# A quantised FFN on one NeuronCore: rounding offset carried through fp32 transposes, conversions off GpSimd, VectorE's order rewritten

## The chip, the cores and the metric

One Trainium2 chip, one of its cores. The metric is device time in microseconds of one execution of the whole program; lower is better.

## The reference, cut to what matters

Two batches of 512 tokens, width 128. Four residual steps follow each other: a cross attention to a context of 77 rows (16 heads of 64), a quantised gated FFN, a second transformer block (`a1`, causal self attention with 16 heads of 32, its own FFN, then `a2`, a second cross attention with its FFN) and a last FFN with a gate. The change is in the FFN of the first block and in what comes right behind it:

```python
def _act_quant(x):
    scale = 127.0 / jnp.clip(jnp.max(jnp.abs(x), axis=-1, keepdims=True), 1e-05)
    xq = jnp.clip(jnp.round(x * scale), -128.0, 127.0) / scale
def _bitlinear(x, w):            # weights are rounded to -1, 0, 1 times a mean
    return einsum('bsi,oi->bso', _act_quant(x), _weight_quant(w))
gate = silu(_bitlinear(x, w_gate)); up = _bitlinear(x, w_up)
out = _bitlinear(gate * up, w_down)
...
x = x + tanh(g_ffn[0]) * _L0_ffn_ref(_layernorm(x), w_gate, w_up, w_down)
x1 = _ln(_layernorm(x), ln1_g, ln1_b)      # then a1: xn = _ln(x1, lnx_g, lnx_b), yn = _ln(x1, lny_g, lny_b)
```

## The kernel before

Every engine has an instruction order written out by hand; semaphores join them. Tokens lie on the 128 partitions in four tiles (NT) per batch (NB = 2), so the quantised FFN has eight hidden tiles of 128 tokens by 512. PSUM has eight banks, S0 to S3, T0, T1, A and B. `claim` makes TensorE wait until the last reader of a bank is done, `await_bank` lets a reader wait for its filling, `release` marks it read.

Rounding is done by adding MAGIC = 1.5 * 2^23, which leaves an integer plus that offset in fp32.

**x of the FFN.** VectorE normalises (`ln_norm("f0", b)`) and takes the largest magnitude (`scale_x`, L1549). ScalarE multiplies by its inverse and adds MAGIC (`round_x`, L1115, four instructions of 128x128), then subtracts it into bf16 (`x_to_bf16`). TensorE transposes in bf16 (`xq_transposes`), ScalarE copies the result out (`xq_evac`). For batch 0 this happens at the end of the cross attention `cross("l0")`, whose 16 units run in a loop over i with the units' steps at i, i+1, i+2 and i+3; for batch 1 inside the FFN.

**Hidden tile n.** TensorE: `gate_up(n)`, two matmuls of 128x512 into the bank pair S0, S1 (n even) or S2, S3 (n odd). ScalarE: `silu(n)`. VectorE: the product with the up half into `h_in` (L1597), its largest magnitude (L1606), clip (L1602) and inverse (L1609); clip and inverse of tile n-1 stand in between those of tile n. ScalarE: scale and MAGIC (L1213). GpSimd: MAGIC off, to bf16 (L1021). TensorE: four bf16 transposes into T0 or T1 (L688). ScalarE: copy out (L1209). TensorE: four matmuls with `w_down` into A (batch 0) or B (batch 1) (L680). VectorE: `f0_out(b)`, scale and residual (L1566), for batch 0 before tile 7.

**Behind it, batch 0.** VectorE: statistics of ln1, affine norm in two passes of four instructions (L1357, L1361), statistics and norm of a1 (L1348). The variance's power is on GpSimd (`power`, L988). TensorE: `ln_transposes("a1", 0)` into A; ScalarE evacuates it twice, with the affine of x and of y (`a1_evac`); four projections of two matmuls (L711), whose high halves ScalarE takes (L1224) and low halves VectorE (L1628); the halves go through DMAs into `stack`, in the order in which the heads need them. Four value projections (L784) follow, then the attention loop over 32 heads: scores (L725), maximum (VectorE, L1691), exponential (ScalarE, L1265), mask of the diagonal block (GpSimd, L1032), transposes of the weights (L444), copies (L1250, L1655), values (L761). The second batch's `f0_out(1)` and ln1 statistics stand before the low halves, its affine norm (`ln1_gain`, `ln1_bias`, L1368 and L1375) before the loop, its a1 statistics and norm on VectorE inside it (n = 0 and n = 2).

`keep_busy(count, res)` (L460) issues matmuls of 128x512 that nobody reads, after waiting for the last reader of the bank `res`.

Of the kernel before, what the change touches and what calls it, by code (L numbers as in the profile page):

```python
# [33 lines left out]
BF16 = mybir.dt.bfloat16  # L34
# [48 lines left out]
def build(nc, x, ctx_in, w64, w128, wf0, wa1, wa2, wa2kv, wf1, rows, cols, out):  # L83
    with ExitStack() as st:
# [32 lines left out]
        def context_heads(start, n_tiles):  # L117
# [16 lines left out]
        xqb, xqT = (pring[:, s, k, :].bitcast(BF16).rearrange("p (b n) -> p b n", b=NB)  # L134
                    for s, k in ((0, 3), (1, 2)))
# [4 lines left out]
        hqb = hid[:, 1, 2:3, :].rearrange("p a n -> p (a n)").bitcast(BF16).rearrange("p (s n) -> p s n", s=2)  # L140
# [26 lines left out]
        rstd = sb("rstd", [P, NB, NT])  # L167
        cstats, cmv, cvar, crstd = (sb("cstats", [M, NB, 6]), sb("cmv", [M, NB, 2]),
# [55 lines left out]
        xq_ready, xqT_ready = sem("xq_ready"), sem("xqT_ready")  # L224
# [4 lines left out]
        hq_ready, hqT_ready = sem("hq_ready"), sem("hqT_ready")  # L229
# [210 lines left out]
        def _(pe):  # L440
# [6 lines left out]
            def ln_transposes(site, b):  # L447
                res = "AB"[b]
                claim(pe, res, ("ln", site, b), read_by=(ynT_ready, b + 1) if site == "a1" else
# [73 lines left out]
            def xq_transposes(b):  # L523
                pe.wait_ge(xq_ready, b + 1)
                res = ("A", "T0")[b]
                claim(pe, res, ("xq", b), read_by=(xqT_ready, b + 1))
                for t in range(NT):
                    m = pe.transpose(bank16(res)[:, t * P:(t + 1) * P], xqb[:, b, t * P:(t + 1) * P], identb[:, :])
                filled(m, ("xq", b))

            def cross(site):
# [5 lines left out]
                for i in range(NU + 3):  # L537
# [20 lines left out]
                    if site == "l0" and i == 2:  # L558
                        for n in range(len(VO_GROUPS)):
                            transpose_values("l0", 0, n, VO_BANKS["l0"][n])  # L560
                    if i >= 3:
# [33 lines left out]
                    if site == "l0" and i == NU + 1:  # L595
                        xq_transposes(0)
                        pe.wait_ge(wq_ready, 2)
                        gate_up(0)
# [68 lines left out]
            gate_up(1)  # L667
            for n in range(NB * NT + 4):
                if 1 <= n < NB * NT - 1:
                    gate_up(n + 1)  # L670
                if n >= 4:
                    j = n - 4
                    b, t = j // NT, j % NT
                    pe.wait_ge(hqT_ready, j + 1)
                    res = out_bank("f0", b)
                    if t == 0:
                        pe.wait_ge(wq_ready, 3)
# [1183 lines left out]
```

## Time and profile before

| | us |
|---|---|
| median of 3 runs | 370.52 |
| lowest and highest of them | 370.10, 373.45 |
| the profiled execution | 370.13 |
| its span, first to last instruction | 368.4 |

Busy over that span: TensorE 325.3, VectorE 287.4, ScalarE 271.0, GpSimd 122.7 us; mean granted TensorE clock 0.977. All durations below are from that one execution, and its time is 0.39 us below the median. PE is TensorE, PEld its weight loads, DVE VectorE, ACT ScalarE, POOL GpSimd, SP the queue that issues the DMAs; L1597 is line 1597 of the kernel. A bracket at a row's end is the engine's idle time before the row and what ended it.

### The profile page before, as it was taken

To read this page: it belongs to the slowest core of one execution; us is meant where nothing else is said; L and a number is where in the kernel's file an instruction comes from. 1 tells how busy PE (TensorE), PEld (TensorE's weight loads), DVE (VectorE), ACT (ScalarE), POOL (GpSimd) and SP (SyncE) were. 2 spreads that over 40 slices of the span, in tenths; PEclk is the share of its full clock that TensorE was granted. 3 is DMA by queue.
4 is the path that set the end of the run, shared out by engine and by line. 5 is a ranking of instruction groups with operands and counts; after the bars stand their busy time and mean duration, and the time that the engine had idled before them with its cause. 6 is when DMAs were issued, how large, how long until landed. Compare 5 with 4: busy or idle time off the path is not lost. (4 is left out here: it accounts for less than half of the span.)

```text
span 368.4 us, 6956 instructions
## 1 busy us (share of the span) xinstructions
PE 325.3 (88%) x2168; PEld 231.1 (63%) x2168; DVE 287.4 (78%) x738; ACT 271.0 (74%) x957; POOL 122.7 (33%) x227
## 2 busy tenths in 40 slices
PE   4989999636699788989989999989899899999997
PEld 4867988513344545655555566757566688877775
DVE  0768768787878998979898998985678887976545
ACT  2378899738445999999898999972545998892463
POOL 1316575324630332323232333331012454441110
PEclk9999999976799999999999999999999999999999
DMA  6900000000008969800992398400000000000001
GB/s 199 377 16 1 2 1 2 0 1 2 2 0 186 206 137 204 182 3 1 199 209 52 71 209 179 174 3 0 2 0 3 0 3 0 4 0 2 0 0 59
DMA packets 7052, 24.75 MB, mean 67 GB/s; under 512 B 1467, under 2 KB 1800, under 8 KB 6280
## 3 DMA queue, kind: packets, MB, share of 16 engines
q1 hardware_dynamic: 7016, 24.31, 27.4%
q8 instruction: 18, 0.29, 0.3%
q14 instruction: 18, 0.15, 0.1%
HBM read 7.00 MB, written 0.52 MB: 20 GB/s over the span
## 5 line engine op out<-in xcount | busy, mean ns | idle before, releaser
L1265 ACT ACTIVATE pring<-ps,nm 128x512 f32<-128x512 f32 x128 | 88.7, 721 | 6.7 <-DVE nm L1691 6.7
L1691 DVE TENSOR_REDUCE nm<-ps 128x1 f32<-128x512 f32 x128 | 80.9, 677 | 9.9 <-PE ps L725 9.7
L1144 ACT ACTIVATE arena<-ps,nmx 128x77 f32<-128x77 f32 x256 | 79.1, 346 | 11.4 <-DVE nmx L1443 11.1
L1032 POOL TENSOR_SCALAR_AFFINE_SELECT pring<-pring 128x128 f32<-128x128 f32 x128 | 37.2, 293 | 79.4 <-ACT pring L1265 79.4
L1144 ACT ACTIVATION_READ_ACCUMULATOR arena<-ps,nmx 128x1 f32 x256 | 58.2, 227 | 0.0
L725 PE MATMUL ps<-stack 128*128 128x512 f32 x128 | 53.4, 480 | 4.2 <-ACT pring L1265 3.6
L997 POOL TENSOR_TENSOR arena<-arena,rden 128x616 f32<-128x616 f32 x32 | 39.2, 1225 | 50.2 <-DVE rden L1452 50.2
L444 PE MATMUL ps<-ident,pring 128*128 128x128 f32 x320 | 47.6, 276 | 6.2 <-ACT early L1237 1.9
L444 PEld LDWEIGHTS ps<-ident,pring 128*128 128x128 f32 x320 | 36.2, 140 | 22.0 <-POOL pring L1032 11.7
L571 PEld LDWEIGHTS ps<-arena 128*128 128x128 f32 x320 | 38.9, 191 | 12.6 <-DVE arena L1459 11.2
L571 PE MATMUL ps<-arena 128*128 128x128 f32 x320 | 42.5, 280 | 3.3 <-DVE arena L1459 3.2
L988 POOL TENSOR_TENSOR rstd<-var,minus_half 128x4 f32<-128x4 f32 x18 | 19.1, 1062 | 76.9 <-DVE var L1341 76.8
L547 PE MATMUL ps<-arena,xnT 128*128 128x308 f32 x128 | 38.9, 427 | 1.7 <-ACT arena L1144 0.7
L725 PEld LDWEIGHTS ps<-stack 128*128 128x128 f32 x128 | 21.5, 189 | 25.5 <-ACT pring L1265 18.6
L1459 DVE COPY arena<-ps 128x384 f32<-128x384 f32 x64 | 28.2, 480 | 11.1 <-PE ps L444 11.1
L1250 ACT ACTIVATE arena<-ps 128x512 f32<-128x512 f32 (+1 forms) x48 | 28.4, 593 | 5.1 <-PE ps L444 5.1
L1443 DVE TENSOR_REDUCE nmx<-ps 128x8 f32<-128x616 f32 x32 | 25.5, 796 | 6.8 <-PE ps L547 6.4
L1265 ACT ACTIVATION_READ_ACCUMULATOR pring<-ps,nm 128x1 f32 x128 | 30.6, 239 | 0.0
L444 PE MATMUL ps<-ident,arena 128*128 128x128 f32 x200 | 27.5, 273 | 0.9 <-DVE arena L1419 0.5
L1168 ACT ACTIVATE hid<-ps,cols_sb 128x512 f32<-128x512 f32 x24 | 16.2, 685 | 15.6 <-PE ps L616 15.6
L1655 DVE COPY arena<-ps 128x384 f32<-128x384 f32 x48 | 26.2, 546 | 1.3 <-PE ps L444 1.2
L547 PEld LDWEIGHTS ps<-arena,xnT 128*128 128x128 f32 x128 | 21.7, 189 | 8.3 <-issue 1.9
(151 smaller groups left out, 527.3 us busy)
## 6 DMA issues: line engine op xcount, KB each, us to landing
stack<-sides SPq DMA_DIRECT2D x32, 256.0 KB, 5.2
stack<-arena SPq DMA_DIRECT2D x16, 256.0 KB, 5.0
stack<-hid SPq DMA_DIRECT2D x12, 256.0 KB, 5.3
wa_sb<-in_wa SPq DMA_DIRECT2D x1, 1536.0 KB, 13.5
early<-in_w SPq DMA_DIRECT2D x2, 512.0 KB, 7.7
stack<-hid SPq DMA_DIRECT2D x8, 128.0 KB, 2.5
arena<-in_wa SPq DMA_DIRECT2D x1, 1024.0 KB, 5.1
pring<-in_wf SPq DMA_DIRECT2D x1, 768.0 KB, 10.0
```

Of the source, the lines that this page charges most:

```text
L444: m = pe.transpose(bank(res)[0:width, t * parts:(t + 1) * parts], src(t), ident[0:parts, 0:parts])
L547: m = pe.matmul(bank(res)[:, 0:4 * HS].rearrange("p (h s) -> p h s", s=HS)[:, :, 0:M], xnT[:, b, t * P:(t + 1) * P], FK[:, b, c0:c0 + 4 * ...
L571: m = pe.matmul(bank(res)[:, t * P:(t + 1) * P], PTc[:, j % 4, k, :], VO[:, b, half * (NCH // 2) + k, :], start=(half == 0 and k == 0), st ...
L725: filled(pe.matmul(bank(f"S{i}"), stack[:, j, 0, e, i * P:(i + 1) * P], stack[:, j, 1, e, :], start=True, stop=True), ("s1", n, i))
L997: pool.tensor_tensor(pv, pv, rden[:, j % 4, :].unsqueeze(2).to_broadcast([P, 8, M]), ALU.mult).then_inc(pn_ready, 1)
L1032: pool.affine_select(out=blk, in_=blk, compare_op=ALU.is_gt, fill=0.0, base=0, pattern=[[1, P]], channel_multiplier=-1).then_inc(masked, 1)
L1144: ins = act.activation(Pc[:, i % PC_SLOTS, h * HS:h * HS + M], bank(where[key])[:, h % 4 * HS:h % 4 * HS + M], ACT.Exp, bias=nmx[:, i % 4, ...
L1250: release(act.activation(pt_piece(n, piece), src, ACT.Copy), key)
L1265: release(act.activation(pring[:, n % 2, i, :], bank(f"S{i}"), ACT.Exp, bias=nm1[:, n % 8, i:i + 1], accum_out=den1[:, n % 8, i:i + 1]), ( ...
L1459: release(dve.tensor_copy(PTc[:, j % 4, k0:k1, :].rearrange("p k n -> p (k n)"), bank(res)[:, 0:(k1 - k0) * P]), key)
L1655: release(dve.tensor_copy(pt_piece(n, piece), src), key)
L1691: dve.tensor_reduce(nm1[:, n % 8, i:i + 1], bank(f"S{i}"), AX.X, ALU.max, negate=True).then_inc(nm1_ready, 1)
```

## The change

- The offset stays: x and the hidden tiles keep MAGIC through transposes that are now fp32, from `xn` and `h_in`, and ScalarE takes it off in the copy out of PSUM, to bf16. `x_to_bf16` and GpSimd's L1021 go; the buffers `xqb` and `hqb` go.
- `round_x` moves from ScalarE to GpSimd: after j = 13 of `cross("l0")` for batch 0, after the power for batch 1.
- In `cross("l0")` VectorE does the second step of `l0_out(0)`, statistics, norm and scaling at i = 11, 12, 13, 14 instead of 12, 13 and 14, 15, 15; TensorE transposes x at the start of i = 16, and the first `gate_up` stands at the start of i = 17.
- The loop over hidden tiles is written out on each engine. VectorE: tile 6 behind ln1 and a1's statistics, tile 7 behind the a1 norm, `f0_out(1)` and its statistics behind the four low halves. TensorE: tiles 6 and 7 between the a1 transposes and the projections, `keep_busy` in other places.
- a1 norm of batch 0 is transposed twice, into A and S1; ScalarE evacuates x, VectorE y.
- GpSimd takes batch 1's ln1 norm with its affine (`ln1_affine`, six instructions and a negation of the mean) ahead of its first mask, and a1's norm of batch 1 behind head 2. VectorE's a1 statistics of batch 1 move from head 0 to head 1.

```diff
+            def hidden_transposes(n):
+                pe.wait_ge(hround_ready, n + 1)
+                res = f"T{n % 2}"
+                claim(pe, res, ("hq", n), read_by=(hqT_ready, n + 1))
+                transposes(("hq", n), res, lambda k: h_in[:, n % 4, k * P:(k + 1) * P], NF)
...
+            gate_up(2)
+            hidden_transposes(0)
+            keep_busy(3, "B")
+            gate_up(3)
+            f0_down(0)
+            hidden_transposes(1)
+            keep_busy(4, "B")
+            xq_transposes(1)
+            f0_down(1)
+            gate_up(4)
+            hidden_transposes(2)
+            gate_up(5)
+            hidden_transposes(3)
+            f0_down(2)
+            f0_down(3)
+            gate_up(6)
+            hidden_transposes(4)
+            f0_down(4)
+            gate_up(7)
+            hidden_transposes(5)
+            f0_down(5)
+            keep_busy(6, "S3")
...
+            hidden_transposes(6)
+            keep_busy(4, "A")
             ln_transposes("a1", 0)
-            keep_busy(4)
-            for m in range(4):
-                project(m, ("S0", "S2", "A", "B")[m])
-            for t, res in enumerate(("T0", "T1", "S1", "S3")):
+            claim(pe, "S1", "a1_context", read_by=(ynT_ready, 1))
+            transposes("a1_context", "S1", lambda t: xn[:, 0, t, :], NT)
+            f0_down(6)
+            project(0, "S0")
+            project(1, "S2")
+            hidden_transposes(7)
+            project(2, "S1")
+            f0_down(7)
+            project(3, "S3")
+            for t, res in enumerate(("T0", "T1", "A", "T0")):
                 project_values(t, res)
             keep_busy(6, "S0")
...
+            def round_x(b):
+                pool.wait_ge(xscale_ready, b + 1)
+                for t in range(NT):
+                    ins = pool.tensor_scalar(xn[:, b, t, :], xn[:, b, t, :], ainv[:, b, t:t + 1], MAGIC,
+                                             ALU.mult, ALU.add)
+                ins.then_inc(xround_ready, 1)
+            def negate_mean(site, b):
+                pool.wait_ge(var_ready, nth(site, b))
+                pool.tensor_scalar(nmean[:, b, :], mv[:, b, :, 0], -1.0, 0.0, ALU.mult, ALU.add)\
+                    .then_inc(nmean_ready, 1)
+            def ln_norm(site, b, src, dst):
+                pool.wait_ge(nmean_ready, negated[0])
+                pool.wait_ge(rstd_ready, nth(site, b))
+                for t in range(NT):
+                    ins = pool.tensor_scalar(dst[:, b, t, :], src[:, b, t, :], nmean[:, b, t:t + 1],
+                                             rstd[:, b, t:t + 1], ALU.add, ALU.mult)
+            def ln1_affine(b):
+                x1_b = x1[:, b, :, :]
+                ln_norm("ln1", b, r, x1).then_inc(ln1_step, 1)
+                pool.wait_ge(ln1_step, 1)
+                pool.tensor_tensor(x1_b, x1_b, row4("ln1_g"), ALU.mult).then_inc(ln1_step, 1)
+                pool.wait_ge(ln1_step, 2)
+                pool.tensor_tensor(x1_b, x1_b, row4("ln1_b"), ALU.add).then_inc(xn_ready, 1)
...
             power("f0", batches=[1])
-            for j in range(NB * NT):
-                pool.wait_ge(hround_ready, j + 1)
...
-                pool.tensor_scalar(hqb[:, j % 2, :], h_in[:, j % 4, :], MAGIC, None, ALU.subtract).then_inc(hq_ready, 1)
-                if j == 5:
-                    power("ln1", batches=[0])
+            round_x(1)
+            power("ln1", batches=[0])
             power("a1", batches=[0])
+            negate_mean("ln1", 1)
             power("ln1", batches=[1])
+            ln1_affine(1)
...
+            for n in range(7):
                 if n == 2:
                     xq_evac(1)
+                round_hidden(n)
+                if n + 2 < NB * NT:
+                    silu(n + 2)
+                if n < 6:
+                    hidden_evac(n)
...
+            ln_evac("a1", 0, ("a1_lnx_g", "a1_lnx_b"))
+            hidden_evac(6)
+            high_half(0)
+            high_half(1)
+            round_hidden(7)
+            high_half(2)
+            hidden_evac(7)
+            high_half(3)
+            copy_values(0)
             preload(ACT.Exp)
-            copy_values(0)
             copy_values(2)
...
+            hidden_behind(5)
+            hidden_scale_alone(5)
+            f0_out(0)
+            ln_stats("ln1", 0, r)
             ln_norm("ln1", 0, r, ("ln1_g", "ln1_b"), x1)
+            ln_stats("a1", 0, x1)
+            hidden(6)
+            hidden_max(6)
+            hidden_scale_alone(6)
+            ln_norm("a1", 0, x1)
+            hidden(7)
+            await_bank(dve, "a1_context")
+            release(dve.tensor_scalar(ynT[:, 0, :], bank("S1"), col("a1_lny_g"), col("a1_lny_b"), ALU.mult, ALU.add),
+                    "a1_context")
+            hidden_max(7)
+            hidden_scale_alone(7)
...
+            for m in range(4):
+                low_half(m)
             f0_out(1)
             ln_stats("ln1", 1, r)
-            for m in range(4):
-                low_half(m)
             copy_values(1)
             copy_values(3)
-            ln1_gain(1)
-            ln1_bias(1)
```

## Rows read from the trace of the kernel before

**Rows 1.** Windows: PE, PEld, DVE, ACT, POOL busy (instructions), clock, DMA share, GB/s.
```profile
...
80.00:90.00 10.00, 4.17 (x24) 2.09 (x23) 7.88 (x24) 7.43 (x15) 4.06 (x3) 0.55 0.00 0
90.00:100.00 10.00, 6.14 (x42) 2.94 (x43) 8.74 (x33) 6.30 (x11) 6.99 (x6) 0.79 0.01 3
...
120.00:130.00 10.00, 8.12 (x41) 5.04 (x39) 9.84 (x25) 8.80 (x25) 3.77 (x11) 1.00 1.00 211
...
```

**Rows 2.** Windows of 2 us, same columns.
```profile
...
78.00:80.00 2.00, 0.58 (x1) 0.10 (x1) 1.88 (x9) 0.00 (x0) 1.01 (x1) 0.69 0.01 4
...
96.00:98.00 2.00, 0.69 (x2) 0.28 (x3) 1.92 (x9) 0.00 (x0) 1.04 (x1) 0.50 0.00 0
...
102.00:104.00 2.00, 1.68 (x16) 1.17 (x16) 0.79 (x7) 0.60 (x1) 1.11 (x2) 0.83 0.00 0
...
```

**Rows 3.** Timeline of VectorE: start, busy time, line, operation, count, idle before.
```profile
...
76.36 0.75 DVE L1545 SCALAR_TENSOR_TENSOR r<-ps,tg,r 128x512 f32<-128x512 f32 x1
...
83.00 0.74 DVE L1597 SCALAR_TENSOR_TENSOR hid<-ps,du,hid 128x512 f32<-128x512 f32 x1
...
84.52 0.73 DVE L1597 SCALAR_TENSOR_TENSOR hid<-ps,du,hid 128x512 f32<-128x512 f32 x1
...
93.84 1.12 DVE L1566 SCALAR_TENSOR_TENSOR r<-ps,dout,r 128x128 f32<-128x128 f32 x4 [0.83 <-PE ps L680]
...
96.39 0.17 DVE L1341 TENSOR_SCALAR var<-mv 128x4 f32<-128x4 f32 x1
...
98.34 1.47 DVE L1357 SCALAR_TENSOR_TENSOR x<-r,mv,rows_sb 128x128 f32<-128x128 f32 x4
...
104.02 1.11 DVE L1348 TENSOR_SCALAR xn<-x,mv,rstd 128x128 f32<-128x128 f32 x4 [1.16 <-POOL rstd L988]
...
111.14 0.69 DVE L1628 SCALAR_TENSOR_TENSOR hid<-ps,hid 128x512 fp32r<-128x512 f32 x1 [0.17 <-ACT hid L1224]
...
114.55 1.13 DVE L1368 SCALAR_TENSOR_TENSOR x<-r,mv,rows_sb 128x128 f32<-128x128 f32 x4
...
116.89 2.48 DVE L1691 TENSOR_REDUCE nm<-ps 128x1 f32<-128x512 f32 x4
...
```

**Rows 4.** Timeline of TensorE, same columns.
```profile
...
95.27 0.40 PE L680 MATMUL ps<-wf0b,hid 128*128 128x128 bf16 x4 [1.03 <-ACT hid L1209]
95.52 0.40 PE L688 MATMUL ps<-identb,hid 128*128 128x128 bf16 x4
97.31 2.74 PE L464 MATMUL ps<-wf0b,identb 128*128 128x512 bf16 x6 [1.39 <-DVE hid L1597]
...
105.28 0.63 PE L444 MATMUL ps<-ident,xn 128*128 128x128 f32 x4 [0.37 <-DVE xn L1348]
...
106.77 1.12 PE L711 MATMUL ps<-xnT,wa_sb 128*128 128x512 f32 x2
...
109.45 1.02 PE L711 MATMUL ps<-ynT,wa_sb 128*128 128x512 f32 x2
...
114.85 1.27 PE L725 MATMUL ps<-stack 128*128 128x512 f32 x4
...
```

**Rows 5.** Timeline of GpSimd, same columns.
```profile
...
29.81 0.62 POOL L974 TENSOR_SCALAR bo_tg<-rows_sb,tg 128x128 f32<-128x128 f32 x1
...
36.05 1.27 POOL L979 TENSOR_TENSOR r<-r,bo_tg 128x512 f32<-128x512 f32 x1
...
41.31 0.69 POOL L963 TENSOR_SCALAR pring<-pring,winv 128x512 f32<-128x512 f32 x1
...
93.97 1.49 POOL L1021 TENSOR_SCALAR hid<-hid 128x512 bf16<-128x512 f32 x1 [0.18 <-ACT hid L1213]
...
102.95 1.04 POOL L988 TENSOR_TENSOR rstd<-var,minus_half 128x4 f32<-128x4 f32 x1 [0.88 <-DVE var L1341]
...
118.47 0.29 POOL L1032 TENSOR_SCALAR_AFFINE_SELECT pring<-pring 128x128 f32<-128x128 f32 x1 [9.10 <-ACT pring L1265]
...
```

**Rows 6.** Timeline of ScalarE, same columns.
```profile
...
105.94 0.78 ACT L1080 ACTIVATE xnT<-ps,cols_sb 128x512 f32<-128x512 f32 x1 [2.35 <-PE ps L444]
...
107.94 0.60 ACT L1224 ACTIVATE hid<-ps 128x512 fp32r<-128x512 f32 x1 [0.55 <-PE ps L711]
...
117.62 0.69 ACT L1265 ACTIVATE pring<-ps,nm 128x512 f32<-128x512 f32 x1 [3.93 <-DVE nm L1691]
...
121.41 0.69 ACT L1265 ACTIVATE pring<-ps,nm 128x512 f32<-128x512 f32 x1 [0.52 <-DVE nm L1691]
...
```

**Rows 7.** Waits in 66 to 120 us: total, times, longest.
```profile
...
PE ps L464 <- DVE hid L1597: 1.4, 1, 1.4
...
```

More of the change, by code:

```diff
@@ L523, in xq_transposes, with f0_down @@
             def xq_transposes(b):
[L524 to L529, printed above, removed]
+                pe.wait_ge(xround_ready, b + 1)
+                claim(pe, "AB"[b], ("xq", b), read_by=(xqT_ready, b + 1))
+                transposes(("xq", b), "AB"[b], lambda t: xn[:, b, t, :], NT)
+            def hidden_transposes(n):
[3 more added lines that the diff above has]
+                transposes(("hq", n), res, lambda k: h_in[:, n % 4, k * P:(k + 1) * P], NF)
+            def f0_down(n):
+                b, t = n // NT, n % NT
+                pe.wait_ge(hqT_ready, n + 1)
+                res = out_bank("f0", b)
+                if t == 0:
+                    pe.wait_ge(wq_ready, 3)
+                    claim(pe, res, ("out", "f0", b), filled_by=(f0_done, n + NT))
+                for k in range(NF):
+                    m = pe.matmul(bank(res)[:, t * P:(t + 1) * P], hqT[:, n % 2, k * P:(k + 1) * P],
+                                  wf0b[:, 2, k * P:(k + 1) * P], start=(k == 0), stop=(k == NF - 1))
+                filled(m, ("out", "f0", b))
             def cross(site):
@@ L560, in cross @@
                             transpose_values("l0", 0, n, VO_BANKS["l0"][n])
+                    if site == "l0" and i == NU:
+                        xq_transposes(0)
+                    if site == "l0" and i == NU + 1:
+                        pe.wait_ge(wq_ready, 2)
+                        gate_up(0)
                     if i >= 3:
@@ L1002, in cross @@
                         ternary((j - 5) // 2, (j - 5) % 2)
+                    if site == "l0" and j == 11:
+                        power("f0", batches=[0])
                     if site == "l0" and j == 13:
-                        power("f0", batches=[0])
+                        round_x(0)
                     if site == "a2" and j == 2:
@@ L1237, in copy_values @@
                 release(act.activation(V[:, t, :], bank(res), ACT.Copy), key)
-            def a1_evac(b):
-                ln_evac("a1", b, ("a1_lnx_g", "a1_lnx_b"), last=False)
-                ln_evac("a1", b, ("a1_lny_g", "a1_lny_b"), dst=ynT)
             def pt_copy(n, piece):
@@ new lines, in hidden_scale_alone, with hidden_behind @@
+            def hidden_scale_alone(n):
+                hidden_clip(n)
+                settle()
+                hidden_scale(n)
+            def hidden_behind(n):
+                hidden(n)
+                hidden_clip(n - 1)
+                hidden_max(n)
+                hidden_scale(n - 1)
+            hidden(0)
+            hidden_max(0)
+            hidden_scale_alone(0)
+            l0_out(1)
+            ln_stats("f0", 1, r)
+            hidden(1)
+            hidden_max(1)
+            hidden_scale_alone(1)
```

192 lines of the change are left out of this document (63 added, 129 removed).

## The prediction

> **What bounds the kernel now.** I read the windows first. From 120 us on, VectorE and ScalarE are 98% and 88% busy and TensorE 81% [rows 1]: the causal attention runs there, and its start is what everything behind it waits for. In the stretch that the change rewrites no engine is the bound: VectorE is 79% and 87% busy, ScalarE 74% and 63%, TensorE 42% and 61%, GpSimd 41% and 70% [rows 1]. There a chain from engine to engine decides, and TensorE's granted clock shows how idle it is: 0.69 in 78 to 80 us, 0.50 in 96 to 98, back to 0.83 in 102 to 104 [rows 2]. The profile's chain of what ended last only reaches back to 323 us, behind the change, so I followed the timelines, engine by engine, asking at each gap who was late.
>
> In them the middle reads so. VectorE adds cross attention's second batch into `r` at 76.36, paces tiles 2 and 3 of the hidden layer at 1.52 us each (83.00 to 84.52), starts `f0_out(0)` at 93.84, the affine norm of batch 0 at 98.34, the a1 norm at 104.02, the fourth low half at 111.14, batch 1's affine norm at 114.55, and only at 116.89 the first maximum of the attention [rows 3]. TensorE starts the a1 transposes at 105.28 and the fourth projection at 109.45, the first scores at 114.85 [rows 4]. GpSimd's conversion of a hidden tile takes 1.49 us [rows 5], nearly the 1.52 of VectorE, and sits between ScalarE and TensorE in every tile. The first exponential is at 117.62, the first of the second head at 121.41 [rows 6].
>
> I laid each engine's new order out with the durations of such rows, an instruction starting at the later of its engine being free and its last awaited result (0.06 us later). The old order laid out in the same way starts the a1 transposes at 105.26 (105.28 in the trace) and the second head's exponential at 121.39 (121.41), so the method is good to about 0.2 us. Times below are its results for the new order, on the clock of the profiled execution.
>
> **Cross attention's end.** VectorE does `l0_out(0)`, the statistics, the norm and the scaling each one turn earlier, in larger lumps, so the last maximum and the last exponentials are late by about 1 us; but `scale_x` no longer stands before the last reciprocal. The two nearly cancel. TensorE no longer waits there for the transposed x (ready at 69.8), so `hidden(0)` is at 73.4 and `l0_out(1)` at 75.2, 1.2 us earlier than the row at 76.36 [rows 3].
>
> **x of batch 1.** ScalarE's rounding and conversion become one rounding on GpSimd, 4 calls of 128x128. No row shows that call. The nearest by size is one multiplication of 128x128 at 0.62 us, the nearest by form (a scalar per partition and a constant, two operations, fp32) 128x512 at 0.69 [rows 5]. The mask, also 128x128, takes 0.29 [rows 5]. So 4 calls lie between 1.1 and 2.5 us; a second operation has not cost more in these rows, and I take 1.5, nearest to the form. It is on the path (the rounding starts at 81.7): `gate_up(4)` starts at 84.6, and 0.4 us earlier or 2.0 later by the ends for both batches.
>
> **Hidden tiles.** Without GpSimd's 1.49, tiles 4 and 5 follow ScalarE and TensorE; each fp32 quartet of transposes costs 0.6 us instead of 0.4 [rows 4] and is covered except in tiles 6 and 7. Tile 6 is moved behind the norm. `f0_out(0)` starts at 89.8, 4.0 us earlier. From there to the variance's end 2.72 us (93.84 to 96.56 in [rows 3]), to 92.6; the power on GpSimd 1.04 [rows 5], which is now bare, since VectorE's next instruction waits for it; the affine norm, two passes. Of such a pass the row at 98.34 shows 1.47 beside a busy GpSimd, the row at 114.55 1.13 beside an idle one [rows 3, 5]; it is now idle, so 2.3 instead of 3.0. Statistics 1.6 (2.72 less the 1.12 of `f0_out`), tile 6 alone 1.8 (the pace of 1.52 and the 0.3 that a following tile covered), so the a1 norm starts at 99.4: 4.6 us earlier than 104.02. Up to here the change gains.
>
> The Trainium skill (GPSIMD Engine Reference, section 8) says that GpSimd shares SBUF interfaces with VectorE and contends with VectorE instructions that have two SBUF inputs. The trace agrees, 1.47 against 1.13 for that pass; a reader without the page loses nothing of the sum.
>
> **TensorE ahead of the a1 transposes.** Here the gain is lost. `keep_busy(6, "S3")` waits for the last claim of S3, `gate_up(7)`, whose reader is `hidden(7)`; the trace shows that wait, 1.4 us, ended by VectorE's L1597 [rows 7]. The new order has `hidden(7)` behind the a1 norm: it ends at 101.2. TensorE has had nothing since about 94. A gap of that kind brought the clock to 0.50 [rows 2], and the six matmuls then took 2.74 us [rows 4]. So: 101.25 plus 2.6; the transposes of tile 6, queued behind, 0.9; `keep_busy(4, "A")`, 0.9 at the full clock and 1.7 at the low one. The clock came back about 5 us after the six began (97.31, and 0.83 in 102 to 104 [rows 2, 4]), so I take the middle, 1.3. The a1 transposes, ready at 100.5, start at 106.0, against 105.28: +0.7. The second set, into S1 for VectorE, costs 0.45 on TensorE and makes x and y land together.
>
> **From there to the first maximum.** Before: 105.28 to 106.77 to the first projection and to 109.45 to the fourth [rows 4], 1.5 and 2.7 us. After: `f0_down(6)` stands before the first projection and waits for `hidden_evac(6)`, itself behind `ln_evac`: 0.6 (the transposes) + 0.7 (`ln_evac`) + 0.6 (a copy out of a bank) + 0.2 (`f0_down`, whose end needn't be awaited), and the hand-overs, 2.3 us in all [rows 4, 6], to 108.3. Between projections 1 and 2 stand tile 7's transposes, which wait for two high halves and `round_hidden(7)`; between 2 and 3 stands `f0_down(7)`, which waits for `high_half(2)` and `hidden_evac(7)`. From the first projection to the fourth that is 6.1 us, to 114.4. The last low half starts at 116.1 (111.14 before). Then VectorE does what it did earlier before, `f0_out(1)` and statistics, 2.9 us, and two copies, 1.2; batch 1's affine norm (2.3) is gone from it. The first maximum is at 120.9, +4.0. The stack's DMAs start 5.4 us later with the halves that feed them; their slack to the third head (over 3 us) stays.
>
> **GpSimd's queue.** Behind `ln1_affine(1)` stand all masks, and TensorE's first transposes wait for a mask. The variance of batch 1 ends at 119.8; then the negation (128x4: between nothing visible and the power's 1.04, I take 0.35), the power 1.0, 4 calls at 1.5 (again 1.1 to 2.5), and two multiply-adds of 128x512 at 1.27 each [rows 5]. First mask 125.4, against 118.47. ScalarE's copy of the first transposes stands before its next exponential, so the second head starts at 126.9 instead of 121.41: +5.5. VectorE's statistics, moved into head 1, add 0.9 and the norm gone to GpSimd gives back 1.0 by head 4. From then on ScalarE is the bound, with the same work as before, so the shift stays for the rest: **+5.4 us**.
>
> **Sum.** 370.13 (the profiled execution, span 368.4) + 5.4 = 375.5. Its own time lies 0.4 below the median of 370.52, so the forecast is 375.9, 1.5% slower. About 1% is what a measurement of this kernel can tell from no change.
>
> **Rivals.**
> 1. *The keep-busy stretch is cheap.* If the clock is full at 101 us, both stretches and the transposes take 1.3 + 0.45 + 0.9: +3.2 in all, and with GpSimd's calls at 1.1 +2.3, so 372.8 to 373.7. Against it: more than 7 us without TensorE work. For it: little more than guesses on when the clock falls. Other sizes that I overrate by a third would land here as well. Chance 0.22.
> 2. *GpSimd's 128x128 calls cost as its 0.62 row.* +3.0 more (1.0 in each of the roundings and the norm): +8.4, so 378.9. For it: it is the only row of a 128x128 with a scalar per partition. Chance 0.10.
> 3. *The clock is already low from 80 us on.* TensorE now does the transposes in fp32 and two short keep-busy stretches between 76 and 84 us. If it falls as it did at 78 to 80, tiles 1 to 3 take 1.0 us longer: +6.4, so 376.9. The Trainium skill (TensorE: Matmul & The Clock Gate, Part 4) says that transposes do not count as busy in the way matmuls do, which would bring this case about; no row here separates the two. Chance 0.10.
> 4. *It is faster.* The 4.6 us won on VectorE reach the attention if TensorE's path from the norm to the first mask grows by less than that. Its terms are what stands between the norm and the transposes (5.5 us, with `keep_busy`), the hidden layer's steps between the projections (0.8 + 3.4 = 4.2) and GpSimd's lump. Without the first the forecast's +5.4 becomes about nothing, 370.4; with the second hidden as well it is 366.3. It decides at 4.3 us: below that sum of the two the kernel is faster, below 0.6 by over 1%. For it: TensorE, ScalarE and GpSimd have idle time in 90 to 100 us [rows 1]. Against it: each wait stands in a fixed order on its engine. Chance 0.06 for more than 1% faster, 0.05 for near no change.
> A conversion gone from GpSimd that buys nothing, as it is replaced by masks that wait, is part of my forecast and not a rival. My forecast as summed, +4.1 to +6.4: chance 0.47.
>
> **Chances and range.** Slower by over 1% (above 374.2): the forecast and rivals 2 and 3, 0.67. Within 1%: rival 1 and the rest, 0.27. Faster: 0.06. The range 371.2 to 380.0 leaves out the faster case and the worst joint price.
>
> **What would show it.** Right: `f0_out(0)` near 90, the a1 norm's end near 100.5, then the six keep-busy matmuls beginning at the end of `hidden(7)` near 101 at the low clock, the a1 transposes 5 us behind the norm, the fourth projection near 114, the first mask 6 us behind batch 1's variance, ScalarE waiting over 2 us between the first and second head's exponentials, and from the fifth head on the same pace as before. Wrong: a1 transposes within 1 us of the norm, projections 0.9 us apart, a first mask within 2 us of the first exponential, or 128x128 calls on GpSimd outside 0.28 to 0.62 us.

## The result, and the profile after

| | before | after |
|---|---|---|
| median, first measurement (4 runs each) | 371.68 us | 377.95 us |
| ratio, first measurement | | 1.017 (1.009 to 1.024) |
| median, measured again (17 and 4 runs) | 370.54 us | 377.54 us |
| ratio, measured again | | 1.019 (1.017 to 1.020) |
| profiled execution, span | 370.13, 368.4 us | 378.05, 376.3 us |
| busy TensorE, VectorE, ScalarE, GpSimd | 325.3, 287.4, 271.0, 122.7 | 330.3, 285.4, 267.0, 119.5 |

The kernel is 1.9% slower. The forecast was 375.9, 371.2 to 380.0. Four executions in a slower state (379.63 us in experiment 2, 372.95 in experiment 8, two of the kernel before) and three of 466, 789 and 1752 us are left out of the medians and ratios.

VectorE, ScalarE and GpSimd each have 2 to 4 us less work than before, and TensorE 5 us more, part of it at half the clock; the time grew by 6.3 to 7.0. The sum of an engine's work doesn't explain that; the timelines do.

The lines of after that answer to those of before follow, each engine's timeline with the same columns as before. VectorE, against [rows 3]:

```profile
...
74.87 0.75 DVE L1570 SCALAR_TENSOR_TENSOR r<-ps,tg,r 128x512 f32<-128x512 f32 x1
...
91.08 1.13 DVE L1592 SCALAR_TENSOR_TENSOR r<-ps,dout,r 128x128 f32<-128x128 f32 x4
...
94.92 1.14 DVE L1397 SCALAR_TENSOR_TENSOR x<-r,mv,rows_sb 128x128 f32<-128x128 f32 x4 [1.13 <-POOL rstd L1041]
...
100.55 1.10 DVE L1388 TENSOR_SCALAR xn<-x,mv,rstd 128x128 f32<-128x128 f32 x4
101.74 0.75 DVE L1623 SCALAR_TENSOR_TENSOR hid<-ps,du,hid 128x512 f32<-128x512 f32 x1
109.03 0.81 DVE L1683 TENSOR_SCALAR ynT<-ps,cols_sb 128x512 f32<-128x512 f32 x1 [6.54 <-PE ps L444]
...
118.05 0.69 DVE L1695 SCALAR_TENSOR_TENSOR hid<-ps,hid 128x512 fp32r<-128x512 f32 x1 [1.79 <-ACT hid L1263]
...
121.52 0.17 DVE L1381 TENSOR_SCALAR var<-mv 128x4 f32<-128x4 f32 x1
...
122.80 3.67 DVE L1754 TENSOR_REDUCE nm<-ps 128x1 f32<-128x512 f32 x6
...
```

Down to the a1 norm the change wins: `l0_out(1)` is 1.5 us earlier than in [rows 3], `f0_out(0)` 2.8, the a1 norm 3.5. Then comes the row of `ynT` at 109.03, with 6.54 us of idle time in front of it, ended by TensorE: VectorE waits for the a1 transposes. TensorE, against [rows 4]:

```profile
...
102.55 2.74 PE L464 MATMUL ps<-wf0b,identb 128*128 128x512 bf16 x6 [7.38 <-DVE hid L1623]
105.08 1.06 PE L444 MATMUL ps<-ident,hid 128*128 128x128 f32 x4
105.93 1.91 PE L464 MATMUL ps<-wf0b,identb 128*128 128x512 bf16 x4
107.64 1.35 PE L444 MATMUL ps<-ident,xn 128*128 128x128 f32 x8
109.91 0.40 PE L542 MATMUL ps<-wf0b,hid 128*128 128x128 bf16 x4 [0.92 <-ACT hid L1243]
110.15 1.08 PE L721 MATMUL ps<-xnT,wa_sb 128*128 128x512 f32 x2
...
113.38 0.66 PE L444 MATMUL ps<-ident,hid 128*128 128x128 f32 x4 [1.30 <-ACT hid L1235]
...
116.07 0.40 PE L542 MATMUL ps<-wf0b,hid 128*128 128x128 bf16 x4 [1.18 <-ACT hid L1243]
116.31 1.08 PE L721 MATMUL ps<-ynT,wa_sb 128*128 128x512 f32 x2
...
127.87 0.98 PE L444 MATMUL ps<-ident,pring 128*128 128x128 f32 x7 [2.35 <-POOL pring L1083]
...
```

The six matmuls that nobody reads (L464) start when VectorE's last hidden tile is done, after 7.38 us of idle time, at the low clock. Tile 6's transposes and four more unread matmuls follow, and only then the a1 transposes, at 107.64 (105.28 in [rows 4]). The projections, 2.7 us from first to last in [rows 4], take 6.2 here, with two waits for ScalarE between them (1.30 and 1.18) and one of 0.92 ahead of the first. Windows of 2 us over that place; the clock is the third number from the end:

```profile
...
102.00:104.00 2.00, 1.46 (x4) 0.58 (x5) 0.49 (x1) 0.00 (x0) 0.00 (x0) 0.50 0.00 0
104.00:106.00 2.00, 2.00 (x9) 1.24 (x7) 0.00 (x0) 0.00 (x0) 0.00 (x0) 0.50 0.00 0
106.00:108.00 2.00, 2.00 (x7) 0.98 (x6) 0.00 (x0) 0.00 (x0) 0.00 (x0) 0.50 0.00 0
...
```

In 104 to 108 us the other three engines do nothing at all, and TensorE works at half speed, for the most part on matmuls that nobody reads. GpSimd, against [rows 5]:

```profile
...
81.77 1.44 POOL L1005 TENSOR_SCALAR xn<-xn,ainv 128x128 f32<-128x128 f32 x4 [3.46 <-DVE ainv L1581]
...
121.79 0.20 POOL L1014 TENSOR_SCALAR nmean<-mv 128x4 f32<-128x4 f32 x1 [21.93 <-DVE var L1381]
121.94 1.01 POOL L1041 TENSOR_TENSOR rstd<-var,minus_half 128x4 f32<-128x4 f32 x1
123.13 1.74 POOL L1023 TENSOR_SCALAR x<-r,nmean,rstd 128x128 f32<-128x128 f32 x4 [0.18 <-POOL rstd L1041]
124.96 1.27 POOL L1032 TENSOR_TENSOR x<-x,rows_sb 128x512 f32<-128x512 f32 x1
126.30 1.26 POOL L1034 TENSOR_TENSOR x<-x,rows_sb 128x512 f32<-128x512 f32 x1
127.52 1.04 POOL L1083 TENSOR_SCALAR_AFFINE_SELECT pring<-pring 128x128 f32<-128x128 f32 x4
...
```

GpSimd waits 22 us for a variance, and then the whole of batch 1's affine norm stands ahead of the first mask, whose first exponential had come 4 us before. ScalarE, against [rows 6]:

```profile
...
123.52 0.69 ACT L1305 ACTIVATE pring<-ps,nm 128x512 f32<-128x512 f32 x1 [2.64 <-DVE nm L1754]
...
128.56 0.60 ACT L1285 ACTIVATE arena<-ps 128x512 f32<-128x512 f32 x1 [2.26 <-PE ps L444]
129.05 0.68 ACT L1305 ACTIVATE pring<-ps,nm 128x512 f32<-128x512 f32 x1
...
```

The second head's first exponential is at 129.05, 7.6 us later than in [rows 6]. The shift then stays: 7.43 us at the fifth head, 7.49 at the ninth, 7.56 at the 31st, and the span is 7.9 longer.

### The profile page after: what moved, and what is told of

The parts are those of the page before. It is cut to its first block and busy times, and to the rows that moved or that the text cites. A ratio compares the mean times of both kernels' runs of the same rounds, so it can differ in the third digit from the quotient of the medians.

```text
span 376.3 us, 6945 instructions
## 1 busy us (share of the span) xinstructions
PE 330.3 (88%) x2171; PEld 234.5 (62%) x2171; DVE 285.4 (76%) x727; ACT 267.0 (71%) x946; POOL 119.5 (32%) x239
## 5 line engine op out<-in xcount | busy, mean ns | idle before, releaser
L1305 ACT ACTIVATE pring<-ps,nm 128x512 f32<-128x512 f32 x128 | 89.7, 736 | 5.0 <-DVE nm L1754 5.0
L735 PE MATMUL ps<-stack 128*128 128x512 f32 x128 | 55.0, 491 | 1.8 <-ACT pring L1305 0.7
L1305 ACT ACTIVATION_READ_ACCUMULATOR pring<-ps,nm 128x1 f32 x128 | 32.6, 255 | 0.0
L1208 ACT ACTIVATE hid<-ps,cols_sb 128x512 f32<-128x512 f32 x24 | 16.2, 685 | 15.6 <-PE ps L634 15.6
```

The lines of the kernel that those rows point to most:

```text
L735: filled(pe.matmul(bank(f"S{i}"), stack[:, j, 0, e, i * P:(i + 1) * P], stack[:, j, 1, e, :], start=True, stop=True), ("s1", n, i))
L1305: release(act.activation(pring[:, n % 2, i, :], bank(f"S{i}"), ACT.Exp, bias=nm1[:, n % 8, i:i + 1], accum_out=den1[:, n % 8, i:i + 1]), ( ...
```

## The experiments

Each ratio is to the kernel before, run on the same chip, with its 95% interval. "Shift" is the start of the ninth head's first exponential in the profiled execution against before's 151.07. The times of several of these kernels spread over 4 to 5 us and the profile is of a single execution, so a shift says where in a trace the time went, and the median what the edit is worth.

**1. The six matmuls no longer wait for the last hidden tile.**

```diff
-            keep_busy(6, "S3")
+            keep_busy(6, "S2")
```

> The changed kernel with one edit: the six keep-busy matmuls behind tile 5 write bank S2 in place of S3, so they wait for silu(7) (about 94 us) and not for hidden(7) (102.5 us). Theory 1 (the fixed order on TensorE costs): tile 6's transposes start when round_hidden(6) ends, near 101.5 in place of 105.08, four keep-busy matmuls at the low clock follow, and the a1 transposes start near 104 in place of 107.64; the whole is 3.5 us shorter than the changed kernel, about 374.3. Rival (the low clock costs, not the order): without the six matmuls the array is cold for everything that follows, the projections take 1.72 us each in place of 0.86, and the gain is under 1.5 us.

Measured: 374.93 us, ratio 1.012 (1.007 to 1.017), shift +3.8. TensorE:

```profile
...
101.36 1.08 PE L444 MATMUL ps<-ident,hid 128*128 128x128 f32 x4 [5.02 <-issue]
102.24 1.91 PE L464 MATMUL ps<-wf0b,identb 128*128 128x512 bf16 x4
103.95 1.34 PE L444 MATMUL ps<-ident,xn 128*128 128x128 f32 x8
...
```

Nothing but the bank's letter is changed. The six now run in a gap at 95 us, and the a1 transposes come at 103.95 instead of 107.64. Of these 3.7 us about 1.1 are the wait itself (tile 6 was rounded at 101.4 in the first profile, and the six began at 102.55) and 2.5 the six matmuls at the low clock behind it. The theory had 3.5 us in all; the median is 2.6 to 3.0 below the changed kernel's, the shift 3.2 to 3.7.

**2. Neither the six nor the four.**

```diff
-            keep_busy(6, "S3")
...
-            keep_busy(4, "A")
```

> The changed kernel without the six keep-busy matmuls behind tile 5 and without the four behind tile 6. Theory 1: the a1 transposes start right behind tile 6's, near 102.4 in place of 107.64, 5.2 us earlier, and lose 1 to 2 us again because the first projections run at the low clock: 374 or 3 to 4 us less than the changed kernel, no better than with the six matmuls placed early. Rival (the clock decides): the low clock lasts into the value projections (3.6 us at the full clock), and less than 1.5 us is left.

Measured: 373.96 us, ratio 1.009 (1.006 to 1.012), shift +2.9, as the theory had it. TensorE:

```profile
...
101.92 1.09 PE L444 MATMUL ps<-ident,hid 128*128 128x128 f32 x4 [6.32 <-issue]
102.80 1.91 PE L444 MATMUL ps<-ident,xn 128*128 128x128 f32 x8
...
```

a1's transposes now run at the low clock, 1.91 us where experiment 1 had 1.34. That 0.6 us is less than the 1.91 of the four unread matmuls that should have raised the clock. 3 us of the loss are left without any of the ten.

**3. Batch 1's affine norm back on VectorE.**

```diff
-            negate_mean("ln1", 1)
             power("ln1", batches=[1])
-            ln1_affine(1)
...
             copy_values(3)
+            ln1_gain(1)
+            ln1_bias(1)
```

> The changed kernel with batch 1's ln1 norm and affine back on VectorE between the value copies and the attention loop, as before the change; GpSimd keeps batch 1's a1 norm. Theory 1 (lumps trade places): the first maximum is 2.3 us later (near 125.1 in place of 122.80), the first mask follows its exponential within 0.2 us, the second head's first exponential is near 128.4 in place of 129.05: 0.7 us gained, not to be told from nothing by the times. Rival (GpSimd's queue ahead of the masks is the main cause of the loss): 3 us or more gained.

Measured: 377.15 us, ratio 1.016 (1.013 to 1.020), shift +6.3, as the theory had it. GpSimd's lump is gone and the first mask (124.97) stands right behind the first exponential (124.11), but that exponential is late by VectorE's two passes. From the fourth projection to the second head's exponential it is 13.03 us, and 12.74 with the lump on GpSimd. Which engine does it is of no account; that it comes between the projections and the attention is.

**4. Tiles 6 and 7 ahead of everything of a1, on all engines.** TensorE's order; VectorE does `hidden(6)` and `hidden(7)` behind `f0_out(0)`, ScalarE its steps in the same order.

```diff
-            keep_busy(6, "S3")
+            keep_busy(2, "S2")
+            hidden_transposes(6)
+            keep_busy(2, "S2")
+            hidden_transposes(7)
+            f0_down(6)
+            f0_down(7)
+            keep_busy(4, "S3")
...
-            hidden_transposes(6)
-            keep_busy(4, "A")
             ln_transposes("a1", 0)
```

> The changed kernel with hidden tiles 6 and 7 on VectorE right behind ln1's statistics of batch 0 (ahead of its affine norm, where VectorE waited 1.13 us for the power), both tiles' TensorE steps ahead of the a1 transposes, and ScalarE in that order too; keep-busy matmuls split 2, 2 and 4. All else is the changed kernel's, the late f0_out(1) and GpSimd's affine with it. Theory 1: the a1 norm starts near 101.8 (1.2 us later than in the changed kernel, as tile 6 no longer covers the second power), but the a1 transposes start near 103 in place of 107.64 and the fourth projection 4.1 us behind them in place of 8.7; the first maximum is near 113.5 in place of 122.80, and the time is 9 us less: 369, 1 to 2 us under the kernel before. Rival (fp32 transposes or the low clock in 80 to 88 us are the cause): f0_out(0) and all behind it keep their lateness, under 3 us gained.

Measured: 370.35 us, ratio 0.999 (0.995 to 1.002), shift −1.0. The loss is undone, but the 1 to 2 us under the kernel before that were expected aren't there. TensorE:

```profile
...
103.00 1.07 PE L444 MATMUL ps<-ident,xn 128*128 128x128 f32 x8 [0.24 <-DVE xn L1383]
...
107.18 1.02 PE L727 MATMUL ps<-ynT,wa_sb 128*128 128x512 f32 x2
...
118.67 1.75 PE L444 MATMUL ps<-ident,pring 128*128 128x128 f32 x7 [2.33 <-POOL pring L1084]
...
```

The a1 transposes now start 0.24 us after VectorE's norm, and the fourth projection 4.2 us behind them instead of 8.7. The first exponential is at 114.33, 3.3 us earlier than in [rows 6], but the first mask (118.32) still stands behind GpSimd's affine norm, and most of the 3.3 is lost there: the second head's exponential is at 120.31, 1.1 ahead of before.

**5. The offset alone**, with every order as before: ScalarE still rounds x, VectorE does both affine norms.

```diff
-                pool.tensor_scalar(hqb[:, j % 2, :], h_in[:, j % 4, :], MAGIC, None, ALU.subtract)
...
-                        m = pe.transpose(bank16(f"T{j % 2}")..., hqb..., identb[:, :])
+                    transposes(("hq", j), f"T{j % 2}", lambda k: h_in[:, j % 4, k * P:(k + 1) * P], NF)
```

> The kernel before with one part of the change alone: x and the hidden tiles keep their offset through fp32 transposes, and GpSimd's conversion of the hidden tiles and ScalarE's of x are gone; every order is the old one, ScalarE rounds x, VectorE does both affine norms. My theory (the order and what stands between the engines decide, not the conversion): VectorE paces the hidden tiles at 1.5 us as before, f0_out(0) starts at 93.8 as before, the affine norm is no longer beside a busy GpSimd and gains 0.7, which TensorE's queue ahead of the a1 transposes swallows: a1 transposes at 105.3, second head's exponential at 121.4, time within 0.5 us of the kernel before (ratio 0.998 to 1.001). Rival (the conversion taken off GpSimd is itself worth something): a1 transposes 1 us or more earlier, time 1.0 to 1.5 us lower. Other rival (fp32 transposes are dear or let the clock fall): time 1 us or more higher, and the windows of 80 to 90 us at a lower clock than before.

Measured: 370.35 us, ratio 0.997 (0.994 to 1.000), shift +0.1; the second head's exponential at 121.49. VectorE's affine norm and a1 norm:

```profile
...
99.15 1.12 DVE L1335 SCALAR_TENSOR_TENSOR x<-r,mv,rows_sb 128x128 f32<-128x128 f32 x4
...
104.10 1.11 DVE L1326 TENSOR_SCALAR xn<-x,mv,rstd 128x128 f32<-128x128 f32 x4 [1.12 <-POOL rstd L981]
...
```

The pass is 1.12 us instead of 1.47 now that GpSimd is idle beside it, and from `f0_out(0)` to the a1 norm it is 9.45 us instead of 10.18. But `f0_out(0)` came 0.8 later than in [rows 3] and than expected (94.65), so the a1 norm is where it was. Tile 2 still started as before (83.05, 83.00 in [rows 3]); the 0.8 comes at tiles 4 to 6. VectorE can't write tile 4 before TensorE has transposed tile 0 out of the same buffer and waits 1.93 us there, where it waited 1.53 before, and the clock was at 0.50 up to 90 us, in the kernel before at 0.75 in 88 to 90. The two parts of this edit, the conversion taken off GpSimd and the transposes in fp32, are measured together only: as a pair, in the old order, they are worth nothing in time, so they don't make the changed kernel's loss by themselves. What each is worth alone isn't shown.

**6. `f0_out(1)` and its statistics ahead of y's copy**, on top of experiment 4.

```diff
             ln_norm("a1", 0, x1)
+            f0_out(1)
+            ln_stats("ln1", 1, r)
             await_bank(dve, "a1_context")
...
-            f0_out(1)
-            ln_stats("ln1", 1, r)
```

> The run with tiles 6 and 7 first on all engines (370.7), with f0_out(1) and its statistics also ahead of the evacuation of y on VectorE. In that run batch 1's variance ended at 112.3, GpSimd's affine norm followed, and the first mask at 118.3 stood 3.9 us behind the first exponential, TensorE idle 2.3. Theory (what still holds the attention back there is GpSimd's lump, which hangs on that variance): the variance ends near 107.5, the first mask comes down to 1 us behind the first exponential, y's copy is late by 2.9 us and moves the projections that need it and the first exponential by some 1 to 2 us, to 115.5 to 116.5; second head's exponential 117.5 to 119 (121.41 before), time 367.5 to 369. Rival (the projections' own chain is the bound, the lump hides): all of it comes later by what y's copy is late, second head at 121 or later, time 371 to 373.

Measured: 369.23 us, ratio 0.997 (0.995 to 0.999), shift −1.6. The variance ends at 105.6 and GpSimd's affine norm at 111.5, so the first mask (115.81) follows the first exponential (114.96) by 0.9 us, and the second head's exponential is at 118.11, 3.3 us ahead of before. Then a new wait takes half of it. TensorE, and windows of 2 us:

```profile
...
121.72 0.70 PE L741 MATMUL ps<-stack 128*128 128x512 f32 x2 [2.82 <-DMA stack<-hid]
...
```

```profile
...
120.00:122.00 2.00, 0.28 (x1) 0.30 (x2) 2.00 (x7) 1.89 (x6) 0.34 (x2) 1.00 0.97 234
122.00:124.00 2.00, 2.00 (x11) 1.78 (x10) 1.93 (x10) 0.85 (x2) 1.28 (x3) 0.61 1.09 223
124.00:126.00 2.00, 2.00 (x7) 1.28 (x6) 1.72 (x4) 1.80 (x6) 0.73 (x3) 0.53 0.92 188
...
```

The third head's scores need the stack's DMAs, which run at 0.97 of the 16 engines and can't start before the projections' halves. They are the bound of that head now, and behind the wait the clock was at 0.61 and 0.53. The lump's part of the theory holds; the time is a little above its 367.5 to 369, as this wait wasn't in it.

**7. `f0_out(1)` into the wait for a1's power, and batch 1's a1 statistics ahead of the attention**, on top of experiment 4; GpSimd's negation and power for them stand ahead of its masks too.

```diff
             ln_stats("a1", 0, x1)
+            f0_out(1)
             ln_norm("a1", 0, x1)
+            ln_stats("ln1", 1, r)
...
             copy_values(1)
+            dve.wait_ge(xn_ready, nth("ln1", 1))
+            ln_stats("a1", 1, x1)
             copy_values(3)
```

> The run with tiles 6 and 7 first, and besides: f0_out(1) between the statistics and the norm of a1 (it fills the wait for the power), the ln1 statistics of batch 1 right behind that norm, the a1 statistics of batch 1 ahead of the attention loop, and GpSimd's negation and power for them ahead of the masks. Theory: a1 transposes near 103.4, fourth projection near 107.8, batch 1's variance ends near 104.8, GpSimd's affine norm near 111, so the first mask stands right behind the first exponential (114.3) and the second head's exponential is at 117.4 (121.41 before). The third and later heads are limited by the DMAs of the stack and gain 3.9 us. Time 366.2 to 366.8, ratio 0.988 to 0.990. Rival (the DMAs of the stack or VectorE in the first heads eat it): second head near 117.4, but the ninth within 2 us of before, time 368.5 to 370.5.

Measured: 372.06 us (367.90 to 373.31), ratio 1.001 (0.997 to 1.004), shift +2.3. A miss: neither the theory's 366.2 to 366.8 nor the rival's second head near 117.4 (119.95) came. The profiled execution took 372.80 us, near the upper end of the twelve. `f0_out(1)` had to wait 1.15 us for `f0_down(7)`, and the a1 norm behind it left TensorE idle for 1.3 us (transposes at 104.20). The clock was 0.50 in 106 to 108 us, and the first two projections took 1.99 and 1.89 us, 1.12 and 1.02 in experiment 8. Behind that the wait for the stack was 4.2 us.

**8. The same with 5 and 6 unread matmuls instead of 3 and 4 behind tiles 0 and 1.**

```diff
-            keep_busy(3, "B")
+            keep_busy(5, "B")
...
-            keep_busy(4, "B")
+            keep_busy(6, "B")
```

> The kernel with f0_out(1) and the affine norm early, with 5 and 6 matmuls instead of 3 and 4 that nobody reads, behind the transposes of hidden tiles 0 and 1. Theory (in the changed kernel the granted clock fell to 0.50 in 82 to 86 us because TensorE idled there between short transposes, and that cost 1.3 us): the clock stays above 0.8 in 80 to 88, f0_out(0) comes 0.7 to 1.3 us earlier and all behind it with it, time 0.5 to 1.3 us below the kernel it is made from. Rival (the added matmuls stand in the way, or the clock falls for the gaps before 80 us): f0_out(0) at the same time or later, time the same or up to 0.6 us higher.

Measured: 369.64 us, ratio 0.997 (0.995 to 1.000), 2.4 below experiment 7 (the intervals of the two overlap), shift −2.6. The clock was 1.00 from 76 to 96 us, and `f0_out(0)` stood 15.1 us behind `l0_out(1)`, 15.6 in experiment 7: 0.5 us, where 0.7 to 1.3 were expected, and experiment 9 has the same 15.1 without the edit. The rest of the difference lies in the two profiled executions: in this one the clock was at 1.00 from 104 us on, ahead of the projections (1.12 and 1.02), and in experiment 7's it fell once more. That the edit does this isn't shown.

**9. The changed kernel again.**

> The changed kernel itself once more, beside five rounds of the kernel before, as its own four executions gave only 1.009 to 1.024. Expected 377.4 (376.0 to 378.5), a ratio of 1.014 to 1.022. In its trace the stretch from l0_out(1) to f0_out(0), whose text is the same in six kernels measured, took 15.1 to 16.2 us, by when the clock was low in it; here it falls in the same range, and the a1 transposes stand 7 us behind the start of the a1 norm in any case.

Measured: 377.54 us (377.05 to 377.59), ratio 1.019 (1.017 to 1.020), shift +7.0. Windows of 2 us, both of which were at 0.50 in the first profile of the same kernel:

```profile
...
82.00:84.00 2.00, 0.49 (x2) 0.12 (x2) 1.83 (x6) 0.13 (x1) 1.44 (x4) 1.00 0.00 0
84.00:86.00 2.00, 1.53 (x12) 0.86 (x13) 1.82 (x5) 1.43 (x3) 0.00 (x0) 1.00 0.00 0
...
```

**10. The changed kernel with the edit of experiment 8.**

> The changed kernel with 5 and 6 matmuls that nobody reads instead of 3 and 4 behind hidden tiles 0 and 1. Theory (the low clock in 80 to 88 us is one part of the error of the forecast, at most 1.1 us of its 2.1): from l0_out(1) to f0_out(0) 15.1 us instead of 16.2, the clock above 0.9 there, the stretch behind it unchanged (the six matmuls still wait for the last hidden tile, at the low clock), ninth head at +6.4 instead of +7.5 against before, time 0.5 to 1.1 us below the changed kernel's. Rival (the clock falls for something that these matmuls don't touch): 15.6 us or more, time the same.

Measured: 377.88 us (377.27 to 378.08), ratio 1.020 (1.018 to 1.021), shift +7.0. The stretch took 15.1 us, as it did in experiment 9 without the edit. So the clock there was no lasting cause, and the theory's gain of 0.5 to 1.1 us didn't come.

**11. Experiment 6 with the edit of experiment 8, and 8 unread matmuls ahead of the third head's scores.**

```diff
+                if n == 2:
+                    keep_busy(8, "S0")
                 if n < NHB:
                     scores(n, 0)
```

> The kernel with tiles 6 and 7 first and f0_out(1) ahead of y's copy (369.2), with 5 and 6 instead of 3 and 4 unread matmuls behind tiles 0 and 1, and 8 of them ahead of the third head's scores, where TensorE waited 2.8 us for a DMA of the stack. Theory (that wait let the clock fall to 0.53 in 122 to 126 us, and with it the gain of the ninth head over before shrank from 2.3 to 1.6 us): the clock stays above 0.9 in 120 to 128, second head near 118.5 (121.41 before), third near 123.6, ninth 2.4 to 2.8 us ahead of before, time 368.0 to 368.7, ratio 0.993 to 0.996. Rival (the DMAs of the stack hold the third head and the added matmuls only stand in their way): ninth head 1.6 us ahead or less, time 369 or more.

Measured: 368.83 us (367.63 to 371.80), ratio 0.996 (0.993 to 0.998), the lowest median of all, though its interval overlaps those of experiments 6 and 8; against the changed kernel's 377.54 it is 8.7 us less. Its mechanism isn't shown, though. The profiled execution, 370.22 us, lies in the upper part of the twelve, shift −0.4 where the theory had −2.4 to −2.8 and the rival −1.6 or less. TensorE in it:

```profile
...
118.84 1.90 PE L464 MATMUL ps<-wf0b,identb 128*128 128x512 bf16 x8
123.00 1.09 PE L741 MATMUL ps<-stack 128*128 128x512 f32 x2 [2.26 <-DMA stack<-hid]
...
```

The stack's data came at 123.00, 14.9 us behind the start of the fourth projection; in experiments 6, 7 and 8 that distance was 13.5, 14.9 and 13.5. The clock fell to 0.50 in 124 to 126 us in spite of the eight matmuls. Whether they or the two edits at tiles 0 and 1 make the 0.4 us between this median and experiment 6's can't be told.

## Why the prediction was right

The direction, the mechanism and the place of each loss are as predicted; the size was 1.4 to 2.2 us short by the two profiles, 1.6 to 2.1 by the medians. The band of the forecast as summed, +4.1 to +6.4, holds the first measurement (+6.3 against the kernel before measured beside it) and not the second (+7.0); the range held by its width on this side. Both profiles of the changed kernel against the chain of the prediction:

| start of | predicted | first profile | experiment 9 |
|---|---|---|---|
| `l0_out(1)` | 75.2 | 74.87 | 75.47 |
| `f0_out(0)` | 89.8 | 91.08 | 90.61 |
| a1 norm | 99.4 | 100.55 | 100.08 |
| a1 transposes | 106.0 | 107.64 | 107.01 |
| first projection | 108.3 | 110.15 | 109.20 |
| fourth projection | 114.4 | 116.31 | 115.36 |
| first maximum | 120.9 | 122.80 | 121.86 |
| first mask | 125.4 | 127.52 | 126.58 |
| second head's exponential | 126.9 | 129.05 | 128.25 |

- **The hidden tiles: the step that was too small.** From `l0_out(1)` to `f0_out(0)` I had 14.6 us; it took 16.2 with a low clock in 82 to 88 us and 15.1 at the full clock. So about half of the error was there before the a1 norm began. Part of it is the clock: rival 3 did occur in the first profile, for 1.1 us, and not in the second. The other 0.5 us is in both, and 0.4 of it comes ahead of batch 1's x: from `l0_out(1)` to GpSimd's rounding VectorE took 6.9 us, and the prediction had 6.5. Behind that VectorE waits for ScalarE's `silu` ahead of tiles 4 and 5, 0.95 and 0.85 us in the first profile and 0.27 and 0.44 in the second; the prediction had these two tiles follow ScalarE and TensorE, and at the full clock it is only 0.2 us off from the start of `gate_up(4)` to `f0_out(0)`. The Trainium skill (TensorE: Matmul & The Clock Gate, Part 4) would lay rival 3 to the transposes, which it says don't count as busy as matmuls do. The traces don't bear that out as the cause here: experiment 9 has the same fp32 transposes with the clock at 1.00 from 76 to 96 us. Whether transposes count less than matmuls no run here can show, as matmuls run between them in all these kernels.
- **The bare power and the affine norm.** Predicted 1.04 and 1.15 per pass, measured 1.13 of idle time and 1.14. The a1 norm begins 9.47 us behind `f0_out(0)` in both profiles; predicted 9.6. Experiment 5 shows the contention on VectorE gone with GpSimd's conversion (1.12 against 1.47).
- **TensorE ahead of the a1 transposes.** Six matmuls, tile 6 and four matmuls: predicted 4.8 us, of which the four were a middle between two clocks. Measured from the first start to the a1 transposes 5.1 in the first profile (clock 0.50 to the end) and 4.5 in experiment 9 (0.79 in the last window). The middle was fair, and rival 1, a full clock, is out. Experiment 1 takes the wait and the six matmuls out of this place and gives 2.6 to 3.0 us of time, experiment 2 takes the four out as well and gives 3.6 to 4.0.
- **Between the projections.** Predicted 6.1, measured 6.16 twice. Experiment 4 takes the hidden steps out of there, and is 3.6 us faster than experiment 2; it moves them ahead of the a1 transposes and keeps eight unread matmuls, so that difference isn't of this stretch alone.
- **GpSimd.** Four calls predicted at 1.5: 1.44 with a constant, 1.74 with two values per partition. The negation 0.20 (0.35), the power 1.01, two passes 1.27 and 1.26. The nearest row by form was the right one to take, and rival 2 (0.62 for each call) is out. First mask 5.8 us behind the end of the variance, predicted 5.6.
- **A constant shift afterwards.** 7.4 to 7.6 from the fifth head to the 31st, and 6.9 to 7.1 in experiment 9. Right.
- **Rival 4, that it is faster.** It named the two stretches on TensorE, and gave 370.4 without the first and 366.3 without both. Experiment 2, without most of the first, gave 374.0; experiment 4, without both, 370.3. The signs are right and the sizes 4 us too hopeful. About two of these are the base that was too low. In experiment 4 the a1 norm also comes 10.9 us behind `f0_out(0)` instead of 9.5, as VectorE now does both tiles ahead of it. The rest is what came next: the first mask waits for GpSimd, and once that is gone (experiment 6) the third head waits for the stack's DMAs. I had written that these start 5.4 us later and that their slack of over 3 us stays. In the changed kernel they start 3.3 us later (113.47 against 110.14 before) and no head up to 200 us waits for them; in experiment 6, whose attention starts 3 us earlier than before, the third head waits 2.8 us.

## What to carry to other kernels

Work that exists only to hold the clock up is an instruction like any other in its queue: a wait for a bank ahead of it stands ahead of all that follows. Here the wait and the six matmuls behind it cost nearly 3 us, which a change of their bank gave back. When the order of one engine is rewritten to fill its holes, ask of each engine what now stands between the last result of the old phase and the first of the next; it was the last two of eight tiles, moved into that place, and the unread matmuls around them that made the loss, and moving them out undid it. And a lump that only has to be done some time should hang on an early result rather than on another engine: moving it from GpSimd to VectorE changed 0.3 us of that stretch, while with its input early the first mask stood 0.9 us behind the first exponential instead of 4.0.

## What the runs showed of the hardware that I had not expected

- The low stretch of TensorE's clock doesn't stand at the same place in every execution of the same text. From 76 to 92 us the kernels of experiments 1 to 4 and 9 have the same instructions. The clock was at 0.50 in 82 to 86 and 0.55 in 86 to 88 in the first profile, in 82 to 84 in experiments 1 and 4, in 82 to 88 in experiment 2, in 86 to 90 in experiment 3, and not at all in experiment 9. It is worth up to 1.1 us, and one profile is no evidence for such a cause.
- A TensorE that waits 2 to 4 us inside the attention can fall back too, and then does its next work at half speed, with other engines at work all the while: 0.53 in 118 to 120 us in experiment 4 behind a wait of 2.33, 0.61 and 0.53 in 122 to 126 in experiment 6 behind one of 2.82. It doesn't each time. In experiment 8 the same wait for the stack left the clock at 1.00:

```profile
...
122.20 0.70 PE L741 MATMUL ps<-stack 128*128 128x512 f32 x2 [2.79 <-DMA stack<-hid]
...
```

```profile
...
122.00:124.00 2.00, 1.80 (x11) 1.39 (x11) 1.30 (x3) 1.02 (x4) 0.39 (x2) 1.00 1.09 221
...
```

- The stack's data came 13.5 us behind the fourth projection in experiments 6 and 8 and 14.9 in 7 and 11. The executions of these kernels spread over 4.2 to 5.4 us, those of the changed kernel, which doesn't wait for the stack, over 0.5 in experiment 9. But they spread over 3.7 in its first measurement, and over 4.0 and 4.6 in experiments 1 and 4, whose profiles show no wait for the stack either. So the stack isn't what spreads them all, and the cause stays open.
